# Layer 3's ternary weights: made by GpSimd between layer 2's attention steps, with thresholds computed ahead of that attention

## The reference

```python
# layer 2: 16-head causal attention (head dimension 16), 8 experts of hidden size 128 (top 2) and a shared one
attn = softmax(where(causal, q @ k.T * hd ** -0.5, lowest)) @ v
routed = sum over e of comb[:, e] * ((silu(xf @ w_gate[e].T) * (xf @ w_up[e].T)) @ w_down[e].T)
# layer 3: ternary weights
def _quantize(w):
    gamma = jnp.mean(jnp.abs(w))
    return jnp.clip(jnp.round(w / (gamma + 1e-8)), -1.0, 1.0)
x1, x2 = x @ _quantize(w1).T, x @ _quantize(w2).T      # w1, w2: 704 x 256
out = (sigmoid(x1) * x2) @ _quantize(w3).T             # w3: 256 x 704
```

## Time and profile before

| | us |
|---|---|
| median of 3 runs | 1023.3 |
| lowest and highest run | 1019.24, 1026.06 |
| span of the profiled execution, first to last instruction | 1016.6 |
| time around the span in the profiled execution | not given; median less span is 6.7 |
| busy in the span: TensorE, weight loads, VectorE, ScalarE, GpSimd | 868.2, 506.2, 572.4, 381.3, 225.2 |
| mean granted TensorE clock, as a share of 2.4 GHz | 0.910 |

### The profile page before, as it was taken

The page is one execution under the profiler, slowest core; times in us unless marked ns, Lnnn a source line. Parts: engine busy times, 40 slices in busy tenths (PEclk is TensorE's granted clock), DMA queues, the critical chain, the costliest instruction groups (busy, mean ns, idle before and its releaser), DMA issues.

```text
span 1016.6 us, 11900 instructions
## 1 busy us (share of the span) xinstructions
PE 868.2 (85%) x4799; PEld 506.2 (50%) x4799; DVE 572.4 (56%) x986; ACT 381.3 (38%) x470; POOL 225.2 (22%) x207
## 2 busy tenths in 40 slices
PE   4991979788899999988589998978999889969897
PEld 2451335444455433334237877623333257868776
DVE  4871656363647777832543345396777427954452
ACT  2410014424243555465242331214555763410331
POOL 2541422401010234111210100400111227810010
PEclk9975679989899999999687998966999989989799
DMA  5599446374833400001500002477100051000001
GB/s 170 194 200 195 198 83 116 66 123 122 128 53 100 64 1 1 2 1 33 183 0 1 1 1 86 103 146 106 23 2 1 1 196 63 1 1 1 1 1 42
DMA packets 33313, 71.32 MB, mean 70 GB/s; under 512 B 5637, under 2 KB 14413, under 8 KB 33254
## 3 DMA queue, kind: packets, MB, share of 16 engines
q1 hardware_dynamic: 33258, 70.56, 30.1%
HBM read 49.27 MB, written 18.48 MB: 67 GB/s over the span
## 4 chain that ended last, share of the span: by engine, by line
PE 63%; DVE 19%; DMA 6%; ACT 5%; issue 4%; SPq 2%; POOL 1%; ACTq 0%; DVEq 0%; POOLq 0%
PE psD L1489 10%; PE psO L1608 10%; PE psO L1489 10%; PE psA L1489 9%; PE psD L1553 9%; DVE mx L1109 8%; PE psA L1571 7%; PE psA L1570 3%; DMA Kr<-d_kn 2%; DVE hid_low L1403 2%; SPq L460 2%; PE psD L1555 2%; ACT Pr L855 2%; PE psA L1521 1%; DVE Kg L1391 1%
## 5 line engine op out<-in xcount | busy, mean ns | idle before, releaser
L1109 DVE TENSOR_REDUCE mx<-psD 128x1 f32<-128x512 f32 (+3 forms) x416 | 258.0, 658 | 157.5 <-PE psD L1555 133.1
L855 ACT ACTIVATE Pr<-psA 128x1024 f32<-128x1024 f32 (+3 forms) x192 | 161.5, 865 | 167.5 <-PE psA L1571 167.0
L730 POOL TENSOR_SCALAR_AFFINE_SELECT Pr<-Pr 128x512 f32<-128x512 f32 x96 | 61.1, 636 | 402.8 <-ACT Pr L855 323.7
L860 ACT ACTIVATE Pr<-psA 128x1024 f32<-128x1024 f32 (+3 forms) x96 | 63.3, 702 | 60.3 <-PE psA L1571 59.9
L1608 PE MATMUL psO<-Pr,Vh 128*32 128x512 f32 (+3 forms) x768 | 80.3, 498 | 3.6 <-POOL Pr L730 3.0
L1553 PE MATMUL psD<-Kr,Qr 80*128 80x512 bf16 (+3 forms) x167 | 51.3, 360 | 35.7 <-issue 20.5
L1555 PE MATMUL psD<-maskq,identb 128*128 128x128 bf16 x349 | 72.5, 232 | 0.0
L1571 PE MATMUL psA<-Qr,Kr 113*128 113x512 f32 (+3 forms) x192 | 67.8, 359 | 0.0
L1553 PE MATMUL psD<-Kg,Qs 96*128 96x512 bf16 (+3 forms) x192 | 57.2, 331 | 5.3 <-DVE mx L1109 2.0
L1553 PE MATMUL psD<-Ks,Qs 96*128 96x512 bf16 (+3 forms) x166 | 54.5, 358 | 4.6 <-DVE mx L1109 3.7
L1553 PEld LDWEIGHTS psD<-Kr,Qr 80*128 80x128 bf16 x167 | 17.1, 105 | 75.6 <-issue 29.5
(11 more groups left out here) (392 smaller groups left out, 1730.0 us busy)
## 6 DMA issues: line engine op xcount, KB each, us to landing
d_qr<-Pr SPq DMA_DIRECT2D x16, 512.0 KB, 3.6
Qr<-d_qr SPq DMA_DIRECT2D x4, 1024.0 KB
Qr2a<-d_qr SPq DMA_DIRECT2D x4, 1024.0 KB, 24.9
Qr2b<-d_qr SPq DMA_DIRECT2D x4, 1024.0 KB, 19.9
Pr<-d_cb SPq DMA_DIRECT2D x8, 512.0 KB, 9.0
Qr<-d_qn SPq DMA_DIRECT2D x12, 256.0 KB, 13.6
Kr<-d_kn SPq DMA_DIRECT2D x12, 256.0 KB, 16.9
Qs<-d_gq SPq DMA_DIRECT2D x24, 128.0 KB
```

The lines of the kernel that those rows point to most:

```text
L730: pool.affine_select(out=block_, in_=block_, pattern=[[0, GH], [1, P]], compare_op=ALU.is_ge, fill=0.0, base=0, channel_multiplier=-1).the ...
L855: act.activation(place[:, h, q0:T], src[:, q0:T], ACT.Exp, scale=score_scale(i)).then_inc(a_drained, 1)
L860: act.activation(place[:, h:h + 2, q0:T], src[:, :, q0 - HALF:HALF], ACT.Exp, scale=score_scale(i)).then_inc(a_drained, 1)
L1109: dve.tensor_reduce(mx[:, j, part, h0:h0 + nh], src, AX, ALU.max).then_inc(d_drained, 1)
```

## The change

`magnitudes` moves ahead of group 8's steps, with a new `cut_thresholds` behind it; the matmul goes behind group 8's `maxima_transpose`, ahead of `expert_weights_transpose`; `quantise` moves to GpSimd, in three instructions, one piece behind every second mask. The rest are the unit numbers that follow from it.

```diff
@@ d_attention, DU
             names = [(f"max{groups[0]}", NMAX), (f"mrow{groups[0]}", 1)]
+            if groups[0] > 0:
+                names.append(("gsum", 1))
...
-            + [("rt2", 1)] + d_attention(GROUPS[2]) + [("gsum", 1), ("up2", 2 * (E + DC))]
+            + [("rt2", 1)] + d_attention(GROUPS[2]) + [("up2", 2 * (E + DC))]
@@ sync
-            sp.wait_ge(d_filled, DU["gsum"] + 2 * 4)
+            sp.wait_ge(d_filled, DU[f"o{LAST}"] + 2 * 4)
@@ gpsimd
+            def quantise(k, v, dst):
+
+                r = v.shape[0]
+                tmp = q_tmp[0:r, 0:v.shape[1]]
+                link(pool.tensor_scalar(tmp, v, gam[0:r, 4 + k:5 + k], None, ALU.is_lt))
+                link(pool.tensor_scalar(dst, v, gam[0:r, 8 + k:9 + k], None, ALU.is_gt))
+                op = pool.tensor_tensor(dst, dst.bitcast(F32), tmp, ALU.subtract)
+                link(op)
+
             for i in GROUPS[2]:
                 for kt in range(NT):
                     mask_exponentials(i, kt)
+                    n = NT * (i - GROUPS[2][0]) + kt
+                    if n == 0:
+                        pool.wait_ge(thresholds, 1)
+                    if n % 2 == 1 and n // 2 < len(pieces):
+                        quantise(*pieces[n // 2])
+            pool.tensor_copy(gam[:, 11:12], gam[:, 10:11]).then_inc(quantised, 1)
@@ scalar
-                    act.wait_ge(d_drained, DU["gsum"] + 2 * (m - 1))
+                    act.wait_ge(d_drained, DU[f"o{LAST}"] + 2 * (m - 1))
@@ vector
+            def cut_thresholds():
+
+                src = take()
+                dve.tensor_copy(gam[:, 4:8], src[:, 0:4]).then_inc(d_drained, 1)
+                dve.wait_ge(d_drained, n[0])
+                link(dve.tensor_tensor(gam[:, 6:7], gam[:, 6:7], gam[:, 7:8], ALU.add))
+                link(dve.tensor_scalar(gam[:, 4:7], gam[:, 4:7], 1.0 / (D * F3), EPS_Q, ALU.mult, ALU.add))
+                link(dve.tensor_scalar(gam[:, 8:11], gam[:, 4:7], 0.5, None, ALU.mult))
+                dve.tensor_scalar(gam[:, 4:7], gam[:, 4:7], -0.5, None, ALU.mult).then_inc(thresholds, 1)
+
...
                 maxima_row(groups[0])
+                if groups[0] > 0:
+                    magnitudes()
+                    cut_thresholds()
                 for i in groups:
...
-                if groups[0] > 0:
-                    magnitudes()
                 outputs(groups[-1])
...
-            src = take()
-            dve.tensor_copy(gam[:, 4:8], src[:, 0:4]).then_inc(d_drained, 1)
...
-                link(dve.tensor_scalar(tmp, v, gam[0:r, 4 + k:5 + k], None, ALU.is_lt))
-                link(dve.scalar_tensor_tensor(dst, v, gam[0:r, 8 + k:9 + k], tmp, ALU.is_gt, ALU.subtract))
...
-                if m < len(pieces):
-                    quantise(*pieces[m])
...
-            dve.tensor_copy(gam[:, 11:12], gam[:, 10:11]).then_inc(quantised, 1)
@@ tensor
                     maxima_transpose(groups[0], GH)
+                    pe.wait_ge(gsum_ready, 1)
+                    pe.matmul(d_unit()[:, 0:4], onesf[:], gam[:, 0:4], start=True, stop=True).then_inc(d_filled, 1)
                     expert_weights_transpose()
...
             attention(GROUPS[2])
-            pe.wait_ge(gsum_ready, 1)
-            pe.matmul(d_unit()[:, 0:4], onesf[:], gam[:, 0:4], start=True, stop=True).then_inc(d_filled, 1)
             pe.wait_ge(d_drained, DU[f"o{LAST}"])
```

More of the change, by code:

```diff
@@ L442, in build @@
         hid_cut = sem("hid_cut")
-        gsum_ready, quantised = sem("gsum_ready"), sem("quantised")
+        gsum_ready, thresholds, quantised = sem("gsum_ready"), sem("thresholds"), sem("quantised")
         gated, cum_ready, y3_ready, stored = sem("gated"), sem("cum_ready"), sem("y3_ready"), sem("stored")
@@ L776, in _ @@
             split(6, A["xnT2"] + 4, done=late_split_done)
+            pieces = [(k, *(t[0:(f3_rows(c) if k == 2 else P), c, :] for t in (w, q)))
+                      for k, (w, q) in enumerate(((w31, q31), (w32, q32), (w33, q33))) for c in range(w.shape[1])]
+            def quantise(k, v, dst):
[5 more added lines that the diff above has]
+                link(op)
             for i in GROUPS[2]:
@@ L1407, in _ @@
                     dve.tensor_tensor(ed_low[:, E // 2:E], w_ed[:, E // 2:E], ed_high[1][:], ALU.subtract).then_inc(ed_split2, 1)
-                if m < len(pieces):
-                    quantise(*pieces[m])
-            assert len(pieces) <= E + DC
-            dve.tensor_copy(gam[:, 11:12], gam[:, 10:11]).then_inc(quantised, 1)
             at("up2")
```

## The result

The changed kernel takes 1027.88 us (median of 20 runs, 1020.61 to 1036.79); the kernel before, run beside it, 1022.88 (20 runs, 1014.88 to 1027.18). The ratio is 1.0055, with a 95% interval of 1.0035 to 1.0075: 5.6 us slower, within 1%. The profiled execution took 1026.18 us with a span of 1024.5, so 1.7 us lie around its span. If as much lay around the span of the execution shown of before, 1016.6, that was one of about 1018.3, a quick one.

What follows compares the result with a forecast made beforehand. It took TensorE to set the pace in the experts' stage and to be busiest in the attention. Terms -6.3 + 5.9 + 5.9 = +5.5 us on the median 1023.3 gave 1028.8 us, own range 1024 to 1034, with rivals 1019 to 1038.

Steps and rivals of the forecast that it cites:

- rival D: Layer 2's attention start: clock rises when it did before, paying back 3 us; with cheap compares 1020.4 us; chance 0.06.
- Part 1, the tail: End of the experts' stage: last `hid_low` takes 1.21 us, not 5.51, shortening TensorE's gap before `down2`: minus 6.3 us.
- may lower it or not: Clock behind the 2.0 us gap before `down2`: staying up would give 0 to 1.9 us more; 0.5 taken.
- taking `quantise` off VectorE gives nothing but the gap: Experts' stage: TensorE sets the pace, so only its final 7.9 us wait for the last `hid_low` can be won.
- Part 2, the front: Start of layer 2's attention: TensorE waits for the magnitudes, scores start at 699, not 693: plus 5.9 us, between 5 and 7.
- no work hides it: plus 5.9: Attention start: TensorE, ScalarE and GpSimd have nothing else to do during the wait, so all 5.9 us count.
- Part 3, the pieces: Ten quantise pieces on GpSimd between attention masks make masks late and TensorE's values wait: plus 5.9 us.
- the walk: Group 8, mask by mask at 6.2 us a piece: masks 2, 4, 6 late by 1.0, 1.1, 3.8 us; sum 5.9.
- TensorE, at 31.4 of 34 us, can win back little; I keep 5.9: Group 8's attention: TensorE is too busy to recover the mask delays, so their summed 5.9 us stand.
- rival A: GpSimd compares in the attention run as cheaply as the cast: 0.5 in place of 5.9 us, 1023.4 us; chance 0.22.
- B: Dear GpSimd compares make GpSimd the bound of group 8: 8.5 us a piece costs 16 us, 1039 us; chance 0.12.
- C: Experts' stage: last `hid_low` again starts behind `w3m_low`, so the tail gives 0: 1035 us; chance 0.10.

Runs made afterwards that it cites:

- run 6: Changed kernel with one of quantise's three instructions behind each mask, and magnitudes moved ahead of the first copy of the routing: 1016.81 us, ratio 0.9936 to the kernel before.
- run 7: Changed kernel with whole pieces behind the masks after which GpSimd had been idle longest: 1020.45 us, ratio 0.9977 to the kernel before.
- run 8: Changed kernel with no piece behind mask 5 of group 8, the later pieces coming one place later: 1030.18 us, ratio 1.0069 to the kernel before.
- run 9: Run 7 with magnitudes moved ahead of the first copy of the routing, as in run 1: 1015.92 us, ratio 0.9937 to the kernel before.
- run 12: Run 7 with an extra unused GpSimd block, as long as a wide piece, behind mask 5 of groups 8 and 9: 1039.98 us, ratio 1.0184.
- run 1: Changed kernel with the magnitudes alone moved, into idle time of VectorE ahead of the first copy of the routing: 1026.07 us, ratio 1.0031 to the kernel before.
- run 4: Changed kernel without the ten pieces; GpSimd copies the raw weights instead, so results differ: 1021.16 us, ratio 0.9966 to the kernel before.
- run 5: Changed kernel with one of quantise's three instructions behind each mask, not all three behind every second: 1023.05 us, ratio 1.0006 to the kernel before.
- run 10: Run 7 with one extra unused GpSimd block, as long as a wide piece, behind mask 5 of group 8: 1026.35 us, ratio 1.0046.
- run 11: Run 7 with one extra unused GpSimd block, as long as a wide piece, behind mask 3 of group 8: 1023.28 us, ratio 1.0020.
- run 3: Kernel before with one added wait, so GpSimd starts `w3m_low` only after the last `hid_low`; quantise stays on VectorE: 1018.79 us, ratio 0.9954.
- run 2: Changed kernel's early magnitudes, matmul and thresholds, but the pieces left on VectorE in the experts' stage: 1026.58 us, ratio 1.0033 to the kernel before.

## Why the prediction was right, and where its terms were off

The forecast was 1028.8 us, +5.5 over the median; measured are +5.6 by the ratio. The waits of all three parts came where they were forecast and nearly as long. What the clock does behind them was left out of the third term and, but for rival D, of the second, and the errors cancelled: that the sum is right to 0.1 us is luck.

**Part 1, the tail: held.** -6.3 was forecast; the trace shows 5.9 less up to `down2` (5.85 was worked out for it without the clock), and -6.9 (by 3.8) comes out of the ratios, the clock's share among it. The clock, for which half a microsecond was taken, stays up behind the 2.06 us gap and gives 1.8 us back within `down2` (40.6 for 42.4 us); behind that it is low for some 3 us longer than before, and from `down2` to the end are 117.6 us in both profiled executions. Ten other traces have the same gap of 2.07 us: in five (runs 6 to 9 and 12) the clock stays up and `down2` takes 40.6 us, in five (runs 1, 4, 5, 10 and 11) it falls and `down2` takes 42.1 to 42.2. Here is one of the latter, run 4, whose `down2` starts at 902.34:

```profile
903.00:905.00 2.00, 2.00 (x10) 1.82 (x9) 0.00 (x0) 0.58 (x1) 2.00 (x1) 0.50 0.00 0
```

So "may lower it or not" is what the traces show, and over the eleven the gap's share is 1.1 us rather than 0.5. The claim that taking `quantise` off VectorE gives nothing but the gap held too: TensorE waits for `hid_low` 7.9 us before, 3.6 in run 3 and 2.1 in the changed kernel, so 4.3 of the 5.8 us come by order alone, with `quantise` still on VectorE.

**Part 2, the front: gross right, net too dear.** The wait is 5.5 us, forecast 5.9. Net it is 3.4, by run 2 and by the trace, for behind the wait the clock came back sooner after the first score. That was rival D, to which I gave 0.06 and for which I had 3 us paid back; 2.1 came. D supposed the clock to rise at the time it did and not after the same work, and so it does: from the end of the row's copy to the rise are 10.4 us before and 9.2 to 11.2 in all nine profiled executions that have the wait, though their scores start 5.5 us later. Of the four runs without it two are the same (10.6 and 11.0, runs 9 and 3), and two rise after 3.6 and 6.1 us (runs 1 and 6); what decides that is open. The step that failed is "no work hides it: plus 5.9", in the tacit part that TensorE then runs as before. (What the early magnitudes take off again is less sharp: 2.4 us in run 1 against the changed kernel, 7.2 in run 6 against run 5, 4.1 in run 9 against run 7, each uncertain by some 3.5 us.)

**Part 3, the pieces: the walk right, its sequel missing.** 5.9 us were forecast, 9.1 (by 3.3) measured. The walk's rows came nearly as worked out: a compare 2.05 us for 2.15, the subtraction 1.52 for 1.7, a wide piece 5.8 for 6.2, a stop for mask 6 of 3.56 for 3.8; masks 2 and 4 stopped TensorE by 0.7 us each, for 1.0 and 1.1; stops in all 4.9. What failed is the sentence "TensorE, at 31.4 of 34 us, can win back little; I keep 5.9", which priced the stop by its length. Behind it the same products ran at 1.2 GHz (granted clock 0.50) for nearly 14 us. I had priced just this for the tail, and for the front in rival D, and not here. Run 10 measures it by itself: 3.1 us of stop cost 6.2 in the stage and 7 in the time. That the places cost and not the work is shown by run 7 (8 us less than the changed kernel, with the same pieces); that it is the stop for mask 6 alone isn't, since run 8, without that stop, is no quicker. Also wrong by that: "group 9 takes 34 us as before" (35.5), and groups 10 and 11, not spoken of, lose 0.9 and 1.1 us, the clock being 0.58 in 810 to 814 us and 0.71 in 814 to 820, in work that had it at 1.00 before; what brought it down there is open.

**The rivals.** A falls: a compare of 704 columns takes 2.05 us, nearer to the tensor-scalar of rows 8 than to its cast. The Trainium skill, "GPSIMD Engine Reference", section "4.1 Engine selection", would have one-input operations run roughly at line rate, which rival A took as near the cast's 1.0 ns a column; here the compare with one tensor input costs 2.91 ns a column (2050 over 704), and the two-input subtraction behind it 2.15, so the measurement decides. B falls by the same row, C by the 1.21 us of `hid_low`, and D is true for the front and smaller than I had it. How the errors cancelled: with the pieces priced rightly the forecast would have been 3.2 us higher, with the front's clock 2.5 lower, with the tail 0.6 lower.

Of the 5.6 us that the change costs, then, nothing is owed to its idea and all to two places. With the magnitudes in VectorE's idle time and the pieces where GpSimd has room, the same change makes the kernel 6.4 us quicker than before (run 9, 0.9937; run 6, with one instruction a mask, is level with it at 0.9936). Most of that has a simpler source: run 3's one line gives 4.7 of it, and the intervals of 0.9937 and 0.9954 don't tell the two apart.

## What to carry to other kernels

Work that is moved to an idle engine is priced by the slots it is put into, not by the engine's busy share: list the idle time behind each instruction of the critical hand-over, and put a block only where it fits (GpSimd was busy 5.09 of 34 us here, and a 5.8 us block in a 2.9 us slot cost 7 us). A stop of TensorE is priced at its length plus what the clock does behind it, read from the trace at the nearest stop of that length, in every term of the sum and not only in one; and where the same gap shows both levels of the clock behind it, as the one before `down2` does, at both. And before an engine is relieved of work because its last instruction is late, look whether that instruction is long, and who started just before it: one order of two instructions was worth 4.7 us, all the rest of the change, at its best places, 1.7 us more, which the intervals don't tell from nothing.

## What the hardware showed that I had not expected

The granted clock answered to stops of TensorE of very different length: behind stops of 3.56 and 3.11 us in the attention it was at 0.50 for 10 to 14 us, in all four traces that have them. But ahead of `down2` a gap of 3.58 us (run 3) brought only 3.4 us of it, and 7.87 us 6.8 (before). Behind the gap of 2.07 us at that place, with the same work on both sides, it fell in five traces and stayed up in six. Around a stop of 0.7 us it fell for some 3 us in run 8 and not in run 11. It fell once more in groups 10 and 11 of the changed kernel and of run 12, where no wait over 1 us stands. So the length of the stop alone doesn't tell; what else decides, these runs don't settle.

At the start of layer 2's attention the clock came back sometimes 2 to 4 and sometimes 8 to 9 us after the first score, in the same instructions: first score to first mask is 9.1 us in the kernel before and in runs 3 and 9, 6.9 and 7.8 in runs 1 and 6, which have no wait either, and 7.0 to 7.7 in the nine with the wait.

And the part of the program ahead of the copy of the row of maxima, the same in eleven of the fourteen kernels, put that copy anywhere between 688.5 and 697.0 us in their profiled executions, more than most of the effects studied; the mean clock ahead of it was 0.91 in the earliest and 0.89 in the latest. A difference of spans between two profiles would have led astray (7.9 us between those of before and after, where the ratio says 5.6).
